# Attention kernel on one core: the weights-times-values products of a unit issued as two pairs

## What is computed

```python
xn = layernorm(x)                                    # x: (8, 512, 128)
# attention, 16 heads of 8 channels
Q, K, V = relu(xn @ Wq + bq), relu(xn @ Wk + bk), relu(xn @ Wv + bv)
scores = einsum("bqhd,bkhd->bhqk", Qh, Kh) / sqrt(8)  # masked keys, causal
attn = softmax(scores)
out = einsum("bhqk,bkhd->bqhd", attn, Vh) + xn
s = gamma * (out - mean) / sqrt(var + eps) + beta
g = silu(feed_forward(xn))                           # 8 experts, two gelus
return x + s * g
```

## Time and profile before

| | |
|---|---|
| Median of 3 runs | 577.16 us (576.87 to 579.24) |
| Profiled execution | 578.02 us, of which the span is 576.2 |
| Mean granted TensorE clock over the span | 0.915 |
| Busy share of the span: PE, DVE, ACT, POOL | 82%, 71%, 56%, 23% |
| Attention units | from 209.4 to 557.9 us of the span |

### The profile page before, as it was taken

One profiled execution on the slowest core, in us unless ns is written; L12 is line 12 of the kernel. 1 busy time (PEld: TensorE's weight loads), 2 busy tenths in 40 slices (PEclk: granted clock), 3 DMA queues, 4 the chain that ended last, 5 costly groups with the idle time before them and its releaser, 6 DMA issues. The chain is left out here.

```text
span 576.2 us, 11623 instructions
## 1 busy us (share of the span) xinstructions
PE 473.2 (82%) x3773; PEld 274.0 (48%) x3773; DVE 406.9 (71%) x988; ACT 324.9 (56%) x670; POOL 130.3 (23%) x359
## 2 busy tenths in 40 slices
PE   0059168999996589999989989999989999989950
PEld 0026146666774245545545545545544545545420
DVE  6899888888842566679768757778767768766420
ACT  0038047789887035666756645666745666655740
POOL 8000000000000110110631620440530350440346
PEclk9999768999999559999999979999988999997995
DMA  8800303333334502122122122122121222220000
GB/s 233 265 0 1 88 4 91 93 91 91 92 91 125 118 8 78 51 48 81 44 84 63 49 64 65 52 60 84 42 60 45 81 60 64 62 62 1 3 19 18
DMA packets 28547, 39.40 MB, mean 68 GB/s; under 512 B 5734, under 2 KB 19942, under 8 KB 28518
## 3 DMA queue, kind: packets, MB, share of 16 engines
q1 hardware_dynamic: 28470, 39.03, 24.2%
q10 hardware_dynamic: 48, 0.01, 0.0%
HBM read 25.91 MB, written 10.49 MB: 63 GB/s over the span
## 5 line engine op out<-in xcount | busy, mean ns | idle before, releaser
L834 DVE TENSOR_REDUCE mx<-banks 128x1 f32<-128x384 f32 (+3 forms) x384 | 213.3, 598 | 86.5 <-PE banks L973 79.4
L938 ACT ACTIVATE pt<-banks 128x512 f32<-128x512 f32 (+2 forms) x384 | 193.3, 527 | 128.7 <-PE banks L992 123.0
L973 PE MATMUL banks<-causal,ident_b 128*128 128x128 bf16 x512 | 108.4, 231 | 0.0
L992 PE MATMUL banks<-causalT,ident_b 128*128 128x128 bf16 x512 | 104.9, 224 | 0.0
L1002 PE MATMUL banks<-pt,vg 128*9 128x512 f32 (+3 forms) x1024 | 96.8, 452 | 0.5 <-ACT pt L938 0.5
L971 PE MATMUL banks<-w_room 73*128 73x512 bf16 (+3 forms) x256 | 74.3, 328 | 10.5 <-DVEq L896 10.4
L990 PE MATMUL banks<-q_odd,k_odd 76*128 76x512 bf16 (+3 forms) x256 | 73.6, 317 | 6.2 <-issue 5.1
L990 PE MATMUL banks<-w_room 76*128 76x512 bf16 (+3 forms) x256 | 72.0, 307 | 6.8 <-issue 4.2
L971 PE MATMUL banks<-k_odd,q_odd 73*128 73x512 bf16 (+3 forms) x256 | 73.9, 321 | 0.0
L748 POOL TENSOR_SCALAR mneg<-mx 128x16 f32<-128x16 f32 x32 | 8.1, 252 | 208.2 <-DVEq L842 208.2
L973 PEld LDWEIGHTS banks<-causal,ident_b 128*128 128x128 bf16 x512 | 52.8, 103 | 0.0
(11 more groups left out here) (143 smaller groups left out, 624.4 us busy)
## 6 DMA issues: line engine op xcount, KB each, us to landing
k_scratch<-parts SPq DMA_DIRECT2D x40, 128.0 KB, 2.3
w_room<-q_scratch SPq DMA_DIRECT2D x48, 96.0 KB
w_room<-k_scratch SPq DMA_DIRECT2D x48, 96.0 KB
q_odd<-q_scratch SPq DMA_DIRECT2D x48, 96.0 KB
k_odd<-k_scratch SPq DMA_DIRECT2D x48, 96.0 KB
q_scratch<-parts SPq DMA_DIRECT2D x24, 128.0 KB, 2.3
w_room<-in_w_dram SPq DMA_DIRECT2D x1, 2048.0 KB, 9.5
xn_all<-xn_st SPq DMA_DIRECT2D x8, 256.0 KB, 2.4
```

What stands on the lines that cost most here:

```text
L834: ins = dve.tensor_reduce(mx[:, u % 2, heads[0]:heads[-1] + 1, q], banks[:, S0 + c % RING, 0:w * len(heads)].rearrange("p (h k) -> p h k", ...
L938: act.activation(weights(k, heads[0], len(heads)), banks[:, ST0 + j % RING, 0:(T - P * k) * len(heads)], ACT.Exp, scale=SCALE).then_inc(ex ...
L973: ins = mm(o[:, w - P:w], ident_b[:, :], causal[:, :], start=False, stop=True)
L992: ins = mm(o[:, 0:P], ident_b[:, :], causalT[:, :], start=False, stop=True)
```

## The change

Three things in the second stage. V2 and V3 of the unit before are both issued in step 2, V2 first. V0 and V1 of the unit are both issued in step 10. ACT's copy of `OT` stands behind the exponential of block 3 instead of block 2. Nothing is added or removed: the same 1024 float32 matmuls run on the same operands, and the waits in the code are the same.

```diff
@@ ACT, batch @@
-                            if j == 2 and not (first and g == 0):
+                            if j == 3 and not (first and g == 0):
                                 output(tok)
                             if j == 3 and not (last and g == NG - 1):
                                 maxima(tok, g + 1)
@@ PE, batch @@
                         for j in range(NCH):
                             keys(tok, par, g, j)
-                            if behind and j in (0, 2):
-                                values(prev, 2 + j // 2)
-                            if j == 6:
+                            if behind and j == 2:
+                                values(prev, 2)
+                                values(prev, 3)
+                            if j == 10:
                                 values(g, 0)
-                            if j == 10:
                                 values(g, 1)
```

## The result

The changed kernel takes 551.14 us, the median of 4 runs (550.77 to 551.40), beside 578.20 for the kernel before in the same batch: a ratio of 0.9527, 95% interval 0.9492 to 0.9561. Its profiled execution took 551.3 us, 549.5 of it the span, with a mean granted clock of 0.936 instead of 0.915.

The account below looks back on a forecast made before the run. PE's array was taken to set the pace. Joins 12.4, less late reduces 3.7, plus sequence ends 6.5 and clock 13.8, made 29.0 us off the profiled 578.0: 549.0, or 548.2 counted from the median; range 544.5 to 564.

Parts of the forecast that it names:

- one fall that remains: Attention stage: one or two of the three clock falls remain, giving 552.8 or 557.4 us; chance 0.09.
- The cost of a switch: PE entering and leaving narrow strips: each pairing takes 0.98 instead of 1.19 us, saving 0.21.
- The joins as a sum: All pairings on PE's array: 59 x 0.21 = 12.4 us gained.
- ACT's copy, priced at nothing: ACT's copy moved behind exponential 3: counted as no cost, at most 0.1 us a unit.
- The late reduces: Second units of seven sequences: PE waits 0.33 and 0.20 for DVE's reduces; 3.7 us lost, between 2 and 6.
- The ends of sequences: PE's idle times between sequences: each shrinks by 1.0 as reduce 8 and the resets come earlier; 6.5 us gained.
- The clock: Attention stage: three falls to the lower clock, 4.6 us each, vanish with the long idle times; 13.8 us gained.
- tail: Last two units, where ACT paces: V0's later place and saved switches cancel; zero, within 1 us either way.
- the falls that stay: Rival, attention stage: the clock falls have their own rhythm or come from thin pairs; 562 us, chance 0.14.
- the resets that aren't hidden: Rival, ends of sequences: PE's sequencer stops at the pair's full queue, idle times and falls stay; 568.5 us, chance 0.06.
- bare loads at the join: Rival, inside each pair: the second product's weight loads don't overlap, 7.1 us less gain; 555 us, chance 0.01.
- reduces that set the pace: Rival, all units: reduces come about 0.6 us later than walked, so PE waits; 587 us, chance 0.04.

Follow-up runs that it names:

- the second pair alone: Kernel before with V2 moved down to V3 in step 2, nothing else: 551.35 us, ratio 0.9535.
- the two with the shift and unpaired order: Kernel before with one tiny POOL operation ahead of `mix_out`'s four: 559.15 us; the same plus eight semaphore instructions on PE's sequencer: 575.07 us.

## Why the prediction was right

The forecast was 548.2, with a range of 544.5 to 564; the time is 551.1, inside it. The number alone would not decide: it is nearer to the 552.8 of one fall that remains than to the forecast. The trace does, since no fall is left. Step by step:

**The cost of a switch** held. One pairing alone gives 0.22 or 0.23 a unit in two kernels (10.05 to 9.83 or 9.82), where I took 0.21. **The joins as a sum** were too high: 12.4 forecast, 29.5 units x 0.37 = 10.9 by the saving measured in ordinary units. The term that was wrong is ACT's copy, priced at nothing, at most 0.1 a unit: it costs 0.07 (the kernel with the copy back: 9.60), which the bound held but the value taken did not.

**The late reduces** held: I forecast waits of 0.33 and 0.20 in the second units, 0.53 together; 0.34 and 0.18 were measured. A second unit is 0.48 longer than an ordinary one, so the six of them in the table cost 2.9. In ordinary units chunk 6 finds reduce 3 done, as walked.

**The ends of sequences** brought more: the seven last units are 15.4 shorter, of which 7 x 0.37 = 2.6 is joins and 5.1 clock (13.8 less the 14.3 - 15 x 0.37 = 8.7 of it that lie in ordinary units). That leaves 7.7, where I had 6.5. PE's idle times are 0.71, 0.68 and 0.58 where they were 1.74, 1.76 and 1.62, and 0.42, 0.32 and 0.35 where they were 1.46 and twice 1.40, as forecast. The mechanism is the one described, and the rows answer to the earlier trace rows:

```profile
328.57 1.26 POOL L780 TENSOR_TENSOR mix<-mix,gate_all 128x512 f32<-128x512 f32 x1 [0.28 <-POOLq L742]
...
329.10 0.76 DVE L850 TENSOR_TENSOR rec<-rec,live_all 128x16 f32<-128x16 f32 x1
330.33 1.29 DVE L834 TENSOR_REDUCE mx<-banks 128x2 f32<-128x512 f32 x2
...
L63 PEldq EVENT_SEMAPHORE  x11: 51/51/51, 331.1 to 332.6; - x11
...
333.25 0.38 PE L990 MATMUL banks<-q_odd,k_odd 76*128 76x512 bf16 x1 [0.71 <-ACT pt L938]
```

L850 stands behind POOL's third operation instead of the fourth, 0.53 after it began (0.52 by the prediction's walk), and the resets begin before PE's last chunk and are over 0.65 before its next matmul. What ends PE's idle time is now the exponential, and no longer the issue of instructions.

**The clock** held: no fall from 222.6 to 533, and the pairs of units that held one are shorter by 6.5 each, of which 4.6 is the clock by the sum that I gave: 13.8.

**Not in the sum** was the start of the stage. The low stretch there ended at 222.6 instead of 218.8, which costs the two units behind the first L980 0.8; and that L980 comes 1.1 later. The other kernels show what it goes with. Where V0 stands in step 6 (before, the second pair alone, the two with the shift and unpaired order), these two units take 21.6 to 22.5, and the low stretch ends 14.5 to 15.9 behind the first L980. In the nine kernels where V0 stands later, with or without a pair, they take 22.9 to 24.2, and the stretch ends 17.9 to 19.9 behind it. So this cost comes with V0's move, and the forecast left it out; how the move prolongs the low stretch is open. When the first L980 comes goes with no part of the change (203.7 to 206.3 in the other kernels). The **tail** was priced at zero; with one unit ahead of it, it is 0.4 longer. The kernel with the second pair alone, where V0 stays in step 6, has it 1.0 shorter than the changed kernel and 0.6 shorter than before: moving V0 costs 1.0 there net, and the second pair gives back 0.6, where I had 1 and 0.8.

Together: 10.4 (joins in the 28 units between start and tail, 0.37 each) - 2.9 (six second units) + 7.7 + 13.8 - 1.9 - 0.4 = 26.7, the difference of the spans. The misses partly cancel: the ends brought 1.2 more than forecast and the reduces took 0.8 less, while the joins brought 2.0 less, the start cost 1.9 and the tail 0.4.

**What I had not seen** is how the parts hang together. I wrote the sum as if the idle times, and with them the falls, fell because V0 left step 6. The second pair alone, of which I expected 571, does the same by 0.22 us, since the kernel before missed a gap between two POOL operations by 0.03. Each of the two pairs alone, V0's move without pairing, and one tiny POOL instruction remove all three falls. So the parts don't add up. What V0's move, with the copy's, gives on top of the second pair is 2.3 in ordinary units and 1.9 at the ends, and it costs 2.0 in second units, 1.0 in the tail and 1.2 at the stage's start: nothing in all. Of the rivals, the falls that stay (562), the resets that aren't hidden (568.5), bare loads at the join (555) and reduces that set the pace (587) are all ruled out for this kernel by its trace.

## What to carry to other kernels

Group matmuls of the same narrow shape: each place with narrow strips cost the array about 0.2 us here for the way in and out, and grouping is worth it as long as the engines that the moved work gave time to are not late. When an instruction that is short everywhere is long in one place, look what runs on the engine beside it, and from when: here 0.01 to 0.04 us decided over 1.1 us of waiting, six times over, and through the clock over 14 us more. Before a gain is credited to a reordering, take the coincidence away alone, since a shift by one tiny instruction gave more than half of it here.

## What the runs showed of the hardware

- A VectorE operation on 128x16 elements took 0.17 us alone, and 1.27 when it started 0.03 behind the start of a POOL operation of 128x512 elements (1.26); it ended 0.04 behind that one's end. Started 0.53 or 0.77 behind one, it took 0.76 and 0.53.
- An idle stretch of 1.6 us or more of TensorE at the end of a sequence, in a stream that was otherwise dense, was followed by the lower clock in 7 of 10 places, for 10.2 us in the unpaired orders (five times) and for 3.4 us in the paired one (twice); a stretch of 1.46 us or less there never was.
- A transpose with 48 columns switches like the strips of 9 do: 0.32 us for it from the matmul ahead to the one behind, against 0.11 at 128 columns.
- TensorE's sequencer ran 11 resets (331.1 to 332.6), starting 0.6 before the first matmul behind a pair of products (331.67) and over 1 us before the array's last chunk (332.14).
